# The first layer of an eleven-stage megakernel: an eviction moved from VectorE to ScalarE, a norm in two broadcast operations, and a new order of a batch's work

## The reference

```
x = x + L0_xcond(ctx, layernorm(x), cond)      # 16 heads of 64, 512 queries against 77 context rows and the 512 latents
x = x + L0_ffn(layernorm(x))                   # two ternary-weight products, squared ReLU between
x = x + L1_xcond(layernorm(x), cond, ctx)      # 6 layers of self attention, cross attention and gelu
x = x + L1_ffn(layernorm(x))                   # top-1 of 8 experts
```

```
logits = einsum('bhqd,bhkd->bhqk', q * s, k * s)
w = softmax(logits)                            # over the 512 latent and the 77 context columns together
out = einsum('bhqk,bhkd->bhqd', w, v)
```

## Time and profile before

| | us |
|---|---|
| runs | 2827.35, 2831.61, 2827.07 |
| median of these | 2827.35 |
| the profiled execution | 2819.95 |
| its span, first to last instruction | 2818.2 |
| first batch's row of the first layer on TensorE | 9.43 to 192.04 |
| second batch's row | 192.04 to 374.68 |
| third batch's row | 374.68 to 563.27 |
| fourth batch's row | from 563.27 |

### The profile page before, as it was taken

One profiled execution on the slowest core, in us unless ns is written; L12 is line 12 of the kernel. 1 busy time (PEld: TensorE's weight loads), 2 busy tenths in 40 slices (PEclk: granted clock), 3 DMA queues, 4 the chain that ended last, 5 costly groups with the idle time before them and its releaser, 6 DMA issues.

```text
span 2818.2 us, 45199 instructions
## 1 busy us (share of the span) xinstructions
PE 2503.1 (89%) x16131; PEld 1105.0 (39%) x16138; DVE 2092.2 (74%) x4462; ACT 1820.2 (65%) x3647; POOL 1051.1 (37%) x1322
## 2 busy tenths in 40 slices
PE   6999899998838899999999999999999999997555
PEld 3545454454512233333333333333333333333233
DVE  5778968879647788888888888888888888852133
ACT  3656556555404577777778777887788777883232
POOL 2544535345322334444444444444444444421000
PEclk9999998999858899999999999999999999996677
DMA  2000000000121211221222122212221222100000
GB/s 71 1 1 1 1 1 1 1 34 1 39 58 36 58 53 53 56 60 53 69 56 60 53 69 56 60 53 69 56 60 53 69 56 60 54 22 19 13 0 15
DMA packets 108399, 113.01 MB, mean 40 GB/s; under 512 B 15895, under 2 KB 96909, under 8 KB 107149
## 3 DMA queue, kind: packets, MB, share of 16 engines
q1 hardware_dynamic: 108175, 110.12, 13.7%
HBM read 14.80 MB, written 1.05 MB: 6 GB/s over the span
## 4 chain that ended last, share of the span: by engine, by line
PE 56%; DVE 23%; POOL 6%; issue 6%; SPq 3%; DMA 3%; ACT 3%; DVEq 0%; POOLq 0%; another core or an unknown queue 0%; ACTq 0%
PE psum L863 9%; PE psum L846 6%; DVE A L1326 6%; PE psum L673 5%; PE psum L836 4%; DVE A L1347 4%; PE psum L954 4%; PE psum L773 3%; PE psum L961 3%; PE psum L750 3%; PE psum L741 3%; DVE nm L1200 2%; SPq L578 2%; PE psum L926 2%; PE psum L729 2%
## 5 line engine op out<-in xcount | busy, mean ns | idle before, releaser
L1326 DVE TENSOR_REDUCE A<-psum 128x1 f32<-128x512 f32 x1536 | 1006.1, 685 | 202.4 <-PE psum L846 191.1
L1524 ACT ACTIVATE A<-psum 128x512 f32<-128x512 f32 x1536 | 821.2, 602 | 138.4 <-PE psum L863 79.8
L846 PE MATMUL psum<-A 64*128 64x512 bf16 x1536 | 474.9, 392 | 39.3 <-issue 20.6
L836 PE MATMUL psum<-A 64*128 64x512 bf16 x1536 | 412.7, 387 | 10.7 <-DVE A L1326 6.4
L863 PE MATMUL psum<-A 128*32 128x512 f32 x3072 | 413.2, 610 | 1.0 <-ACT A L1532 0.2
L1658 POOL TENSOR_TENSOR A<-A,rden 128x512 f32<-128x512 f32 x256 | 263.5, 1048 | 364.1 <-DVE rden L1217 364.1
L846 PEld LDWEIGHTS psum<-A 64*128 64x128 bf16 x1536 | 120.2, 95 | 465.2 <-DVE A L1326 388.3
L673 PE MATMUL psum<-ident,A 128*128 128x128 f32 x1280 | 211.9, 294 | 80.9 <-DVE A L1071 38.9
L1471 ACT ACTIVATE A<-psum,nm 128x512 f32<-128x512 f32 x256 | 175.1, 684 | 109.3 <-DVE nm L1203 108.7
L1551 ACT ACTIVATE A<-psum 77x512 f32<-77x512 f32 x384 | 206.3, 592 | 48.1 <-PE psum L917 46.7
L1689 POOL TENSOR_TENSOR A<-A 128x512 f32<-128x512 f32 (+1 forms) x78 | 96.4, 1236 | 346.5 <-DMA A<-A 346.5
(11 more groups left out here) (207 smaller groups left out, 4117.2 us busy)
## 6 DMA issues: line engine op xcount, KB each, us to landing
A<-A SPq DMA_DIRECT2D x456, 128.0 KB, 2.4
A<-A SPq DMA_DIRECT2D x336, 64.0 KB, 2.0
A<-zero SPq DMA_DIRECT2D x60, 128.0 KB, 2.3
wl<-in_wl SPq DMA_DIRECT2D x6, 1024.0 KB, 5.0
A<-A SPq DMA_DIRECT2D x36, 78.0 KB, 2.1
A<-in_nT SPq DMA_DIRECT2D x1, 2304.0 KB, 8.3
A<-in_w SPq DMA_DIRECT2D x2, 512.0 KB, 7.0
A<-in_w SPq DMA_DIRECT2D x1, 1024.0 KB, 6.0
```

Of the source, the lines that this page charges most:

```text
L836: handle.matmul(bank(b), k_st[bt][lo:lo + ROW, h // 2, k * P:(k + 1) * P], q_st[m % 3][lo:lo + ROW, h // 2, :], start=True, stop=True).the ...
L846: handle.matmul(bank(b), q_st[m % 3][lo:lo + ROW, pair, q * P:(q + 1) * P], k_st[bt][lo:lo + ROW, pair, :], start=True, stop=True).then_in ...
L1326: handle.tensor_reduce(nm[:, pair // 4, q, j, pair % 4:pair % 4 + 1], bank(3 + j), AX.X, ALU.max, negate=True).then_inc(mx, 1)
L1524: handle.activation(pT[:, block % 2, i % GROUP, :], bank(ring_of["scores", m, i]), ACT.Exp, scale=HD1 ** -0.5).then_inc(ex, 1)
```

## The change

Three things change, all in the first layer save the norm helper, which the experts use as well.

First, `ctx_turned` goes from VectorE's program to ScalarE's, as an activation with the function Copy of the same 77 x 512 elements; the semaphore is renamed from `tc_d` to `tc_a`.

Second, `centred` no longer issues one tensor_scalar for each of the four blocks of 128 channels (subtract the mean, multiply by the reciprocal root), but one tensor_tensor over all 512 elements that subtracts the mean, broadcast over the channels, and behind it, after a wait on VectorE's own semaphore, one that multiplies.

Third, the four tables of the first layer are new. VectorE's is now 139 long and ScalarE's 159; the other two keep their length.

```diff
-        tr, tr_d, tr_a, tc, tc_d, av, av_a, ow, x0 = (sem(n) for n in ("tr", "tr_d", "tr_a", "tc", "tc_d", "av", "av_a", "ow", "x0"))
+        tr, tr_d, tr_a, tc, tc_a, av, av_a, ow, x0 = (sem(n) for n in ("tr", "tr_d", "tr_a", "tc", "tc_a", "av", "av_a", "ow", "x0"))
...
         VECTOR0 = {
-            "ctx_turned": [-13, -10, 6, 9, 26, 29, 43, 51, 63, 66, 84, 86, 105, 113, 121, 127],
-            "x_norm": 349,
+            "x_norm": 293,
...
-                    owner[4] = (tc_d, 2 * NP0 * bt + i + 1)
+                    owner[4] = (tc_a, 2 * NP0 * bt + i + 1)
...
-                        pe.wait_ge(tc_d, 2 * g + 2)
+                        pe.wait_ge(tc_a, 2 * g + 2)
...
             def centred(src, dst, chain, n, rows):
                 _, mv, _, rs = chain
-                for q in range(n):
-                    t = handle.tensor_scalar(dst[0:rows, q, :], src[0:rows, q, :], mv[0:rows, q, 0:1], rs[0:rows, q:q + 1],
-                                             ALU.subtract, ALU.mult)
-                return t
+                src, dst = src[0:rows, 0:n, :], dst[0:rows, 0:n, :]
+                handle.tensor_tensor(dst, src, mv[0:rows, 0:n, 0:1].to_broadcast([rows, n, D]), ALU.subtract).then_inc(own.next(), 1)
+                after_own()
+                return handle.tensor_tensor(dst, dst, rs[0:rows, 0:n].unsqueeze(2).to_broadcast([rows, n, D]), ALU.mult)
...
-                if name == "ctx_turned":
-                    u, j = divmod(i, 2)
-                    dve.wait_ge(tc, 2 * NP0 * bt + i + 1)
-                    if bt or u:
-                        dve.wait_ge(av, NP0 * bt + u - 1)
-                    handle.tensor_copy(pT0[0:C, u % 2, j, QT, :], psum[0:C, 4, :]).then_inc(tc_d, 1)
...
+                if name == "ctx_turned":
+                    u, j = divmod(i, 2)
+                    act.wait_ge(tc, 2 * NP0 * bt + i + 1)
+                    if bt or u:
+                        act.wait_ge(av, NP0 * bt + u - 1)
+                    handle.activation(pT0[0:C, u % 2, j, QT, :], psum[0:C, 4, :], ACT.Copy).then_inc(tc_a, 1)
```

More of the change, by code:

```diff
@@ L327, in build @@
[L327 to L335 removed]
+                        "exp": [14, 17, 18, 19, 24, 26, 27, 31, 40, 41, 43, 44, 47, 49, 50, 51, 59, 60, 63, 66, 68, 69, 71, 72, 75, 78, 85, 86, 88,
@@ new lines, in build @@
+                90, 99, 103, 106, 109],
+                        "divide": [-37, -34, -31, -28, -16, -14, -10, -8, -1, 2, 5, 8, 13, 19, 22, 28, 30, 34, 38, 45, 50, 54, 60, 61, 67, 70, 74,
+                81, 88, 93, 96, 100],
+            "ctx_max": [-47, -42, -26, -21, -11, -5, 4, 7, 23, 25, 40, 44, 59, 62, 80, 83],
+            "ctx_stats": -125,
+            "x_norm": 293,
+            "b_affine": 157,
+            "b_square2": 159,
+            "b_max": 170,
+            "b_levels": 178,
+            "b_round": 180,
@@ L381, in build @@
+            "ctx_power": 3,
+            "ctx_divide": [41, 53, 61, 75, 84, 92, 103, 112],
+            "lat_power2": 10,
+            "b_power": [124, 125, 149],
+            "x_power": 224,
+            "b_weight": 152,
         }
```

132 lines of the change are left out of this document (58 added, 74 removed).

## The result

| | us, median | runs | ratio to before, 95% interval |
|---|---|---|---|
| before | 2827.24 | 11 | |
| the changed kernel | 2811.43 | 11 | 0.9944 (0.993 to 0.9958) |
| the changed kernel, profiled execution | 2812.83 | 1 | |

The change makes the kernel faster by 15.8 us, 0.56%. The forecast was 2811, 16.4 us less.

What follows compares the result with a forecast made beforehand. TensorE was taken to bound the kernel, except three feed-forward stretches where VectorE sets the pace. Terms 11.5 + 6.8 + 3.9 - 1.8 - 4 gave 16.4 us less, from 2827.35 to 2811, range 2792 to 2836.

Steps and rivals of the forecast that it cites:

- copy off VectorE, less the late copies: First layer's feed-forward stretches: 17 bank 4 copies off VectorE gain 11.5 us, less 4 for copies behind exps on ScalarE.
- norm out of the shadow: waits: Third and fourth rows: last norm no longer beside GpSimd's multiplication, TensorE's waits of 5.26 and 5.0 shrink, 6.8 us gained.
- norm out of the shadow: waits and clock: Same two rows: 6.8 us of waits plus 3.9 us from the 1.2 GHz clock behind them, 10.7 us.
- the other places: First layer's other moves (first scores, GpSimd's power operations, VectorE's statistics) change no work; taken at nothing.
- the norm as a pair: Experts and end of first layer: two broadcast operations 0.3 us longer than four, six times, 1.8 us lost.
- the full stretches: First layer's three 60 us stretches with feed-forward under attention, VectorE 92 to 95% busy; forecast under 90%, TensorE gaps at most 5 us.
- The collision: Third and fourth rows: `x_norm` held up by GpSimd's `b_weight` multiplication, TensorE waiting behind it; removal gains 6.8 us.
- The clock: Behind the two long waits TensorE runs at 1.2 GHz; 3.9 us come back if the waits go.
- The rival with late copies: Bank 4 copy on ScalarE comes late behind exps waiting for maxima, TensorE loses 26 us, 2833 us; chance 0.17.
- the rival in which no bound moves: Feed-forward stretches stay bound by VectorE's bulk operations, only the long waits go, 2.9 us less, 2824 us; chance 0.14.
- all waits for the copy of bank 5 go: First layer, more-than-forecast case: 25.3 us of TensorE's waits for VectorE's copy vanish, 35.4 us gained in all, 2792; chance 0.09.

Runs made afterwards that it cites:

- the late norm: Kernel before with only a batch's last norm six places later in VectorE's table, behind GpSimd's multiplication; ratio 0.9981, 5.4 us shorter.
- copy and late norm: Kernel before, old order, with the bank 4 copy on ScalarE and the last norm behind GpSimd's multiplication; ratio 0.9956, 12.4 us shorter.
- the changed order and four norms: Changed kernel with the old norm of four tensor_scalar operations in place of the two broadcast ones; ratio 0.9938 to before, median 2804.01 us.

## Why the prediction was right, point by point

| term | sum | measured | at one clock, estimate |
|---|---|---|---|
| copy off VectorE, less the late copies | 11.5 - 4 = 7.5 | 6.5 (3.4 to 9.9) | 3.4 (1.9 to 5.0) |
| norm out of the shadow: waits | 6.8 | | -1.7 (-3.2 to -0.3) |
| norm out of the shadow: waits and clock | 6.8 + 3.9 = 10.7 | 5.4 (2.3 to 8.5) | |
| copy and norm together | 18.2 | 12.4 (7.9 to 17) | 5.2 (3.3 to 7.0) |
| the other places | 0 | 5.1, and 10.9 of idle time | 10.8 (8.4 to 13.2) |
| the norm as a pair | -1.8 | -3.1 to -4.8 | -5.1 (-7.0 to -3.3) |
| all | 16.4 | 14.4 and 15.8 | 10.8, and 3.6 by the clock |

**The moved copy: the sign right, the size right only with the clock's part.** By the ratio it is 6.5 us against 7.5, at one clock 3.4. The waits for the moved copy in the changed kernel are 4.0 us, the value taken, though they replace 6.2 us for the same copy on VectorE, and the earlier trace rows showed less than there is: its 0.3 us are those of the matmuls of one line, while TensorE's loads of weights waited 14 us for the same copies of ScalarE, in rows of their own. I had expected VectorE under 90% and TensorE's gaps at 5 us or less in the full stretches. The gaps stay at 26 us in sum with the copy alone, and at 22 us in the changed kernel. I named a check that would have failed a right forecast. And the step behind the 11.5, that work taken off VectorE there "counts there in full", isn't borne out: 17 copies of 0.677 us gave 2 to 4 us of idle time, and the matmuls' waits for VectorE's copy of bank 5 fell from 32.2 us to no less than 26.3.

**The collision: the failed step.** It is "5.26 + 5.0 - 2 x 1.75 = 6.8 us gained", which took a wait's whole length as time. Put back in the new order, 9.9 us of such waits made 3.6 us of idle time; taken out in the old, they changed the idle time not at all, and at one clock the kernel is no shorter. VectorE is held up as the prediction says, but no run shows a gain from the waits themselves. And 1.75 us for what stands in the shadow instead was the lower end: 2.88 us three times in the changed kernel, up to 4.38 in another. I had put 4.5 as the bound and charged the only row that I had.

**The clock: the mechanism holds, and it carried the gain of the late norm.** With the norm out of the shadow in the old order, the slow stretches behind the multiplication go or shrink, and the mean clock of 12 executions is 0.9392 against 0.9355. By the slope that is some 7 us, where the sum had 3.9. In the changed kernel the slow stretches of the earlier trace rows went as well, but the new order has others. Its first profile:

```profile
478.00:483.00 5.00, 2.58 (x15) 1.20 (x13) 4.73 (x8) 3.29 (x9) 2.14 (x3) 0.93 0.00 0
663.60:667.00 3.40, 3.40 (x15) 1.94 (x12) 2.69 (x7) 1.79 (x5) 2.04 (x2) 0.55 0.03 5
673.90:680.70 6.80, 6.80 (x23) 3.02 (x23) 4.96 (x10) 0.00 (x0) 2.90 (x3) 0.53 0.00 0
```

In the whole stretch TensorE's clock is at the slow level for 38 and 58 us in the two profiles of the kernel before, 34 with the late norm, 24 with copy and late norm, and 55 and 44 in the changed kernel. Single profiles spread too far to price this. The clocks of all executions do it better: what is left for the whole change is 0.9375 against 0.9357, some 3.6 us, near the 3.9 of the sum, but as the outcome of slow stretches that went and others that came. The sum had said of those "I count none".

**The places that I took at nothing** are the term that was missing. "The other moves change no work" is true, and yet 10.9 us of TensorE's idle time go with them, and they need the copy on ScalarE to do so. At one clock it is the largest single term of the gain. The order rows in the text ahead showed some of the moves; I had no row from which to price them, and said so, but then gave them no range either.

**The pair** costs more than 1.8 us in the new order: 12 norms in the filled rows were given 4 us for either sign, and the sign is a loss. The expert norm is 1.42 us as forecast.

**Busy times.** VectorE was to lose 40 to 45 us and ScalarE to gain 38. With the copy alone VectorE loses 579.58 - 541.06 = 38.5 and ScalarE gains 444.10 - 415.12 = 29.0, that is 0.60 and 0.45 us a copy, where the rows of single copies have 0.677 and 0.594: an instruction's duration overlaps its neighbours'. The Trainium skill says so too (Perfetto Trace Analysis, "Optimizing Scalar/DVE Operations"): part of the profiled latency of such an instruction lies beside the next. In the whole program VectorE has 2092.2 us before and 2047.2 with the changed order and four norms, 45.0 less, as forecast; the pair puts 9.5 to 10.2 of them back.

In sum, the forecast's number was luck. By the ratios two terms were too large by 5.8 together, one missing by 5.1 and one too small by 1 to 3, and these cancelled. At one clock it is plainer: copy and norm gave 5.2 us where the sum had 14.3 without the clock, and the places, taken at nothing, gave 10.8. The rival with late copies (2833) is refuted. So is the time of the rival in which no bound moves (2824), though VectorE did stay over 90% busy in two of the three stretches, as it says. That all waits for the copy of bank 5 go is refuted too: from 192 us on, 18.4 of 25.3 us are still there.

## What to carry to other kernels

Price a wait on the bounding engine by what its idle time as a whole would lose, not by its length: here waits of 9.9 us were worth 3.6 at most. Price the slow clock behind the wait apart from it, since here that was what paid. When a kernel's runs spread by 0.3%, split a profile into the bounding engine's idle and busy time over the same work, since the first is the kernel's and repeats within 3 us, and the second moves with the granted clock by 10; and compare executions at an equal granted clock, which told here 10.8 us where the medians told 5.1 with intervals that overlap. And when an engine gives work away, the order is to be made anew with it: the same order is worth 5 us with the copy on ScalarE (11 at one clock), and with it on VectorE the kernel was 17 us or more longer than before.

## What the runs showed of the hardware

- VectorE's operations with both inputs in SBUF wait for the end of a GpSimd multiplication however small they are: 128 x 2 elements stood 1.54, 1.76, 2.88, 3.14 and 4.38 us, by when they came. The one that stood longest had come 0.15 us behind the start of the multiplication. A copy and a reduction out of PSUM in the same 4.5 us kept their 0.69 and 1.22 us.
- It goes the other way as well: behind a running VectorE operation, GpSimd's multiplication took 4.94 us in place of 4.50.
- For the same matmuls, TensorE was busy 669.0 us in one execution of one kernel and 678.7 in another, with the idle time at 67.3 and 69.1: a spread of 10 us that the granted clock makes, in a program on one core. The first had 38 us of this stretch at 1.2 GHz, the second 58.
- The time of one kernel goes with its mean granted clock: 2.0 us of 2825 for each 0.001, over 163 executions. An edit after which TensorE waited 2.5 us at most, where it had waited 5.3 and 5.0, raised that mean from 0.9355 to 0.9392.
- An instruction adds less to its engine's busy time than its row shows: 0.60 us for 0.677 on VectorE, 0.45 for 0.594 on ScalarE.
